# A drain between two tiny operations removed, and the start of the kernel reordered, in an attention and feed-forward layer

## The chip, the cores and the metric

The kernel runs on all 8 cores of one Trainium2 chip. Each core takes half the query tiles of one of the four batch entries (every other tile of 128 rows) and reads all keys of that entry that it needs; the cores exchange nothing. The metric is the device time in microseconds of the slowest core. The time before is 1715.69 us, the median of 3 runs (1714.91 to 1715.86).

## The reference, cut to what matters

```python
x = layernorm(x + attn(x, Wq, Wk, Wv, Wo))          # x: (4, 8192, 1024), float32
x = layernorm(x + ffn(x, U1, V1, b1, U2, V2, b2))

attn:  q, k, v = x@Wq, x@Wk, x@Wv;  scores = q @ k^T, causal mask
       softmax(scores / 32) @ v @ Wo
ffn:   gelu(x @ U1 @ V1 + b1) @ U2 @ V2 + b2        # rank 256, hidden width 4096
layernorm: (x - mean) / sqrt(var + 1e-5)
```

## The kernel before

Two products of weights are formed once on each core: M (`m_sb`) from Wq and Wk, and W (`wvo`) from Wv and Wo. With them the scores of a block of 512 queries are z = M x, then z x^T, and the attention's output is (P x) W. Both products are 1024 by 1024 and are computed in two column halves, h = 0 and h = 1, of 8 tiles (e = 0 to 7, 128 rows by 512 columns, 8 matmuls each).

**The start.** SP loads f32 pieces of 512 KB: 16 pieces of Wq and Wk (the list `QK`), 8 of x (own x and the other half of the first block), 16 of Wv and Wo (the list `VO`). ScalarE takes every other piece and casts it to bf16 (`cast`, L759), VectorE takes the rest (L838); their orders are `BY_ACT` and `BY_DVE`. A piece of `VO` from the ninth on reuses the staging place of the piece eight before it, so SP waits for that cast (L430). TensorE forms the first half of M row by row of the weights as they land (`product_by_rows`, L509), the second half tile by tile (`product_by_tiles`, L521), turns 8 tiles of x by transposes for each of the two key chunks (L605, copied out by ScalarE L774 and VectorE L908), then computes z of block 0 (8 tiles, L531), its scores (L547), and the first half of W (L521 again).

**The loop** runs over g = 0 to 7 blocks of 512 queries. Block g meets 2g + 2 key chunks of 512, in the order 2g, 2g + 1, 0, 1, ... (`score_chunks`). In one turn TensorE computes the scores that are left (L547), transposes the probabilities (L563), multiplies with the values (L579) and with W (L652), computes z of the next block (tiles 0 to 5, L531), transposes the first LayerNorm's output (L669), z tile 6, the FFN's first product (L681), z tile 7, the hidden layer (L692, L700), the scores of the next block against its first chunk, and the last product (L722).

**LayerNorm.** VectorE adds the residual to each W tile out of PSUM (L955), takes the statistics of each 128 rows (`statistics`: drain L874, `bn_stats` L876, drain L877, `bn_aggr` L878), and GpSimd computes 1/sqrt(var + eps) from the variance: an add of eps (L362), a drain (L364), a power of -0.5 (L365), each on 128x1 elements. VectorE then waits for it and normalizes (L881). `ln1_out(g, j - 1)` stands in VectorE's program between the residual adds of rows j and j + 1, so that VectorE empties no more W tiles while it waits for GpSimd. TensorE uses 6 PSUM banks as a ring: a new tile has to wait until the tile six before it has been copied out. For the second LayerNorm the statistics and norms are spread over the row maxima of the next block (`ln2_piece`).

**The queues.** Key chunks c >= 2 and all values are f32 in HBM and are cast to bf16 copies in HBM (`xtb`, `xnb`) by DMAs that GpSimd issues (`cast_xt` L329, 1 MB written each; `cast_xn` L332, 2 MB written each). Between L337 and L358 GpSimd first waits for the last casts of `BY_ACT` and `BY_DVE`, then issues, in this order: key chunk 2, the FFN's weights (u1, v1, u2, v2, b1, b2, all counted on one semaphore `d_wf`), key chunk 3, the values of blocks 0 and 1. After the first LayerNorm of block g it issues key chunks 2g + 4 and 2g + 5 and the values of block g + 2 (L371 to L374). SP loads bf16 chunks and values into a ring of five slots of SBUF (`load_scores` L399, `load_values` L405), in order: for block 1 these are chunks 2, 3, 0, 1 and then the values, and each load waits for the cast of what it reads (L398, L449, L450).

The text gives times of core 6, the slowest of the profiled execution.

Of the kernel before, what the change touches and what calls it, by code (L numbers as in the profile page):

```python
# [41 lines left out]
def psum_numbers():  # L42
# [22 lines left out]
    product("m", 0, RB)  # L65
    product("m", 1, 8)
    for c in range(2):
# [3 lines left out]
    for f in range(8):  # L71
        z(0, f)
# [79 lines left out]
def pair_pieces(a, b):  # L152
    out = []
    for i in range(4):
        out += [(a, 2 * i, None), (b, 2 * i, 0), (a, 2 * i + 1, None)]
    return out + [(b, 2 * i, 1) for i in range(4)]


QK = pair_pieces("q", "k")
VO = pair_pieces("v", "o")  # L160
# [6 lines left out]
def build_program():  # L167
# [25 lines left out]
    with ctx:  # L193
# [26 lines left out]
        eps_s = E(nc.sbuf_tensor("eps_s", [128, 1], F32))  # L220
# [29 lines left out]
        d_wf, d_const = S("d_wf"), S("d_const")  # L250
# [73 lines left out]
        def _(g):  # L324
            g.memset(eps_s[:, :], EPS)
# [14 lines left out]
            for k in range(8):  # L340
                g.dma_start(out=u1_sb[:, k * 256:(k + 1) * 256],
                            in_=u1_d.ap()[k * 128:(k + 1) * 128, :]).then_inc(d_wf, 16)
            for rc in range(2):
                g.dma_start(out=v1_sb[:, rc * 4096:(rc + 1) * 4096],
                            in_=v1_d.ap()[rc * 128:(rc + 1) * 128, :]).then_inc(d_wf, 16)
            for fq in range(4):
                g.dma_start(out=u2_sb[:, fq * 2048:(fq + 1) * 2048].rearrange("p (f r) -> p f r", f=8),
                            in_=u2_d.ap()[fq * 1024:(fq + 1) * 1024, :].rearrange(
                                "(f p) r -> p f r", p=128)).then_inc(d_wf, 16)
            for rc in range(2):  # L350
                g.dma_start(out=v2_sb[:, rc * 1024:(rc + 1) * 1024],
                            in_=v2_d.ap()[rc * 128:(rc + 1) * 128, :]).then_inc(d_wf, 16)
            g.dma_start(out=b1_sb[:, :], in_=b1_d.ap()[:, :]).then_inc(d_wf, 16)
            g.dma_start(out=b2_sb[:, :], in_=b2_d.ap()[:, :]).then_inc(d_wf, 16)
# [114 lines left out]
        def _(t):  # L469
# [32 lines left out]
            def product_by_rows(name, lhs, rhs, arrived):  # L502

                banks = [claim((name, 0, e)) for e in range(8)]
                for k in range(8):
                    for p in arrived(k):
                        cast_done(t, p)
                    for e in range(8):
                        mm = t.matmul(ps[banks[e]][:, :],  # L509
                                      lhs[:, k * 1024 + e * 128:k * 1024 + (e + 1) * 128],  # L510
                                      rhs[:, k * 1024:k * 1024 + 512],
                                      start=(k == 0), stop=(k == 7))
                        if k == 7:
                            mm.then_inc(s_full if e < RB else s_acc, 1)

            def product_by_tiles(name, lhs, rhs, h):

                for e in range(8):
# [6 lines left out]
                    mm.then_inc(s_full, 1)  # L525
# [61 lines left out]
            def first_half(a, b):  # L587
                return lambda k: [(a, k, None)] + ([(b, k, 0)] if k % 2 == 0 else [])

            def second_half(b):  # L590
                for i in range(4):
                    cast_done(t, (b, 2 * i, 1))

            product_by_rows("m", wqt, wkt, first_half("q", "k"))
            second_half("k")
            product_by_tiles("m", wqt, wkt, 1)
            t.wait_ge(d_const, 32)
            for c in range(2):
# [22 lines left out]
            for g in range(NG):  # L621
# [19 lines left out]
                if g == 0:  # L641
                    second_half("o")
# [31 lines left out]
                if g == 0:  # L674
                    t.wait_ge(d_wf, 16 * 18)
# [8 lines left out]
                if more:  # L684
                    z_tile(g + 1, 7)

# [21 lines left out]
                for fc in range(32):  # L708
                    hidden(fc)
                    if fc >= 3:  # L710
# [334 lines left out]
```

## Time and profile before

| | |
|---|---|
| time, median of 3 runs | 1715.69 us |
| the profiled execution's own time | 1717.22 us |
| its span on the slowest core (core 6) | 1715.7 us |
| spans of the 8 cores | 1708.8 to 1715.7 us |
| TensorE busy in matmuls | 1573.1 us (92%) |
| VectorE, ScalarE, GpSimd busy | 656.8, 615.3, 112.2 us |
| granted TensorE clock, core 6 | 0.975 of full speed |

Times in the profile count from the start of the core's span. An engine's row gives start, length, engine, line, operation and how many are merged; in brackets stands how long the engine had been idle and which instruction released it. POOL is GpSimd, DVE VectorE, ACT ScalarE, PE TensorE, SPq and POOLq the sequencers of SP and GpSimd. The DMA queue q0 holds what GpSimd issues, q1 what SP issues.

### The profile page before, as it was taken

Reading aid. Unit: us, or ns where it says so; the run is one execution under the profiler, and the core shown is the slowest. Engines: PE = TensorE matmul, PEld = TensorE weight load, DVE = VectorE, ACT = ScalarE, POOL = GpSimd, SP = SyncE. Lnnn points to the kernel's source line nnn. Section 1 sums busy time; section 2 is a strip of 40 time slices with the busy share of each in tenths; the row PEclk is TensorE's granted clock in tenths of the full one; section 3 lists DMA queues with packets and bytes.
Section 4 is the critical chain, followed back from the end, with each engine's and each line's share of the span. In section 5 each row is a group of like instructions: output and inputs, shape, how many; then the busy total and the mean of one; then the engine's idle time right before and its main releaser. Section 6 shows DMA issues by size and latency. Waiting matters only on the chain.

```text
span 1715.7 us, 26161 instructions; the slowest of 8 cores (1708.8 to 1715.7 us)
## 1 busy us (share of the span) xinstructions
PE 1573.1 (92%) x8608; PEld 774.1 (45%) x8608; DVE 656.8 (38%) x1318; ACT 615.3 (36%) x1242; POOL 112.2 (7%) x204
## 2 busy tenths in 40 slices
PE   6991499999999999999999999999999999999985
PEld 2540144444444544445444454444454444455432
DVE  2430325545416432652416440544540515461053
ACT  3510163354074306441074420354420264441023
POOL 0020101110101000100101000100000001000000
PEclk9996699999999999999999999999999999999998
DMA  9999755834665357524575335636335305434301
GB/s 296 306 141 133 131 87 192 164 86 155 202 87 195 106 192 99 167 92 136 200 95 188 132 110 210 110 87 203 129 118 203 134 26 197 148 109 147 137 1 49
DMA packets 72141, 244.55 MB, mean 143 GB/s; under 512 B 4992, under 2 KB 10256, under 8 KB 61328
## 3 DMA queue, kind: packets, MB, share of 16 engines
q1 hardware_dynamic: 60320, 190.86, 32.7%
q0 software_dynamic: 11696, 52.02, 19.6%
q8 instruction: 79, 1.29, 0.3%
q14 instruction: 46, 0.38, 0.1%
HBM read 258.69 MB, written 52.43 MB: 181 GB/s over the span
## 4 chain that ended last, share of the span: by engine, by line
PE 86%; issue 6%; DVE 3%; ACT 2%; DVEq 1%; SPq 1%; DMA 1%; POOLq 0%; POOL 0%; ACTq 0%
PE ps L579 27%; PE ps L547 26%; PE ps L700 7%; PE ps L692 6%; PE ps L531 6%; PE ps L652 5%; PE ps L563 3%; PE ps L521 3%; PE ps L681 2%; PE ps L722 2%; ACT p_sb L808 1%; SPq L423 1%; DMA x_ring<-wkt 1%; DVE p_sb L857 1%; PE ps L669 1%
## 5 line engine op out<-in xcount | busy, mean ns | idle before, releaser
L579 PE MATMUL ps<-p_sb,x_ring 128*128 128x512 bf16 (+2 forms) x2304 | 468.2, 361 | 8.9 <-DVE p_sb L864 5.7
L547 PE MATMUL ps<-x_ring,zt 128*128 128x512 bf16 (+3 forms) x2304 | 465.1, 361 | 0.8 <-ACT zt L732 0.8
L547 PEld LDWEIGHTS ps<-x_ring,zt 128*128 128x128 bf16 x2304 | 220.2, 98 | 235.4 <-issue 1.3
L579 PEld LDWEIGHTS ps<-p_sb,x_ring 128*128 128x128 bf16 x2304 | 216.9, 98 | 235.0 <-issue 11.6
L742 ACT ACTIVATE p_sb<-ps,nm 128x512 bf16<-128x512 f32 (+3 forms) x288 | 187.3, 651 | 264.6 <-DVE nm L846 264.5
L846 DVE TENSOR_REDUCE nm<-ps 128x1 f32<-128x512 f32 (+3 forms) x288 | 184.5, 643 | 202.4 <-PE ps L547 202.4
L823 ACT ACTIVATE p_sb<-ps,b_sb 128x512 bf16<-128x512 f32 x256 | 171.4, 688 | 37.6 <-PE ps L692 35.7
L531 PE MATMUL ps<-x_ring,p_sb 128*128 128x512 bf16 x512 | 116.1, 383 | 60.2 <-DVE x L955 58.7
L700 PE MATMUL ps<-p_sb,wf 128*128 128x512 bf16 x512 | 148.4, 379 | 9.5 <-ACT p_sb L823 9.5
L945 DVE CAST ot<-ps 128x512 bf16<-128x512 f32 x32 | 22.1, 692 | 342.0 <-PE ps L579 342.0
L692 PE MATMUL ps<-p_sb,wf 128*128 128x512 bf16 x512 | 148.5, 379 | 0.6 <-ACT p_sb L732 0.6
L732 ACT ACTIVATE zt<-ps 128x512 bf16<-128x512 f32 x64 | 38.8, 607 | 261.4 <-PE ps L531 261.4
L732 ACT ACTIVATE ot<-ps 128x512 bf16<-128x512 f32 x32 | 19.1, 597 | 287.9 <-PE ps L579 287.9
L970 DVE CAST q_sb<-ps 128x512 bf16<-128x512 f32 x16 | 10.3, 686 | 281.1 <-PE ps L700 281.1
L362 POOL TENSOR_TENSOR vpe<-mv,eps_s 128x1 f32<-128x1 f32 x64 | 22.1, 346 | 1422.6 <-DVE mv L878 1422.6
L793 ACT ACTIVATE p_sb<-ps 128x512 bf16<-128x512 bf16 (+1 forms) x144 | 77.1, 571 | 100.1 <-PE ps L563 100.0
L652 PE MATMUL ps<-wvo,ot 128*128 128x512 bf16 x512 | 111.8, 379 | 1.2 <-DVE wvo L834 1.2
L531 PEld LDWEIGHTS ps<-x_ring,p_sb 128*128 128x128 bf16 x512 | 49.9, 99 | 121.5 <-issue 64.3
L563 PE MATMUL ps<-idb,p_sb 128*128 128x128 bf16 x1056 | 72.5, 219 | 16.7 <-DVE p_sb L857 16.2
L876 DVE BATCH_NORM_STATS2 bst<-x 128x6 f32<-128x512 f32 x128 | 82.3, 685 | 5.8
L857 DVE TENSOR_SCALAR p_sb<-p_sb,fac 128x512 bf16<-128x512 bf16 (+3 forms) x288 | 82.8, 337 | 0.0
L700 PEld LDWEIGHTS ps<-p_sb,wf 128*128 128x128 bf16 x512 | 50.0, 98 | 72.2 <-issue 14.7
(66 smaller groups left out, 955.6 us busy)
## 6 DMA issues: line engine op xcount, KB each, us to landing
x_ring<-xtb SPq DMA_DIRECT2D x70, 1024.0 KB, 6.5
x_ring<-xnb SPq DMA_DIRECT2D x48, 1024.0 KB, 5.4
x<-xo SPq DMA_DIRECT2D x32, 512.0 KB, 8.5
xnb<-xn POOLq DMA_DIRECT2D x8, 2048.0 KB, 35.1
xtb<-xt POOLq DMA_DIRECT2D x14, 1024.0 KB, 18.5
out<-x POOLq DMA_DIRECT2D x28, 512.0 KB, 8.2
x_ring<-xnb SPq DMA_DIRECT2D x16, 768.0 KB, 5.0
x_ring<-xnb SPq DMA_DIRECT2D x16, 512.0 KB, 4.3
```

Source lines behind the costliest of these rows:

```text
L531: mm = t.matmul(ps[b][:, :], m_sb[:, ec * 1024 + f * 128:ec * 1024 + (f + 1) * 128], ring[:, off + ec * 512:off + (ec + 1) * 512], start=( ...
L547: mm = t.matmul(ps[b][:, 0:w], zt[:, ec * 512 + j * 128:ec * 512 + (j + 1) * 128], ring[:, off + ec * 512:off + ec * 512 + w], start=(ec = ...
L563: mm = t.transpose(psb[b][:, k * 128:(k + 1) * 128], P[:, p0:p0 + 128], idb[:, :])
L579: mm = t.matmul(ps[b][:, q0:512], ring[:, off + k * step:off + k * step + 128], P[:, p0 + q0:p0 + 512], start=(c == 0 and k == 0), stop=(c ...
L652: mm = t.matmul(ps[b][:, :], ot[:, e * 512 + j * 128:e * 512 + (j + 1) * 128], wvo[:, e * 1024 + h * 512:e * 1024 + (h + 1) * 512], start= ...
L692: mm = t.matmul(ps[b][:, :], v1_sb[:, rc * 4096 + fc * 128:rc * 4096 + (fc + 1) * 128], p1_sb[:, rc * 512:(rc + 1) * 512], start=(rc == 0) ...
L700: mm = t.matmul(ps[b][:, :], u2_sb[:, fc * 256 + rc * 128:fc * 256 + (rc + 1) * 128], h_sb[:, (fc % 8) * 512:(fc % 8 + 1) * 512], start=(f ...
L742: sc.activation(blocks(c, j, w // 128), b[:, 0:w].rearrange("p (n k) -> p n k", k=128), AF.Exp, bias=nm[:, k:k + 1], scale=1.0, accum_out= ...
L823: sc.activation(h_sb[:, (fc % 8) * 512:(fc % 8 + 1) * 512], b[:, :], AF.Gelu_apprx_tanh, bias=b1_sb[:, fc:fc + 1]).then_inc(out_of["gelu"], 1)
L846: v.tensor_reduce(nm[:, k:k + 1], src[:, 0:width(g, c, j)], AX.X, ALU.max, negate=True).then_inc(s_nm, 1)
L857: v.tensor_scalar(pv, pv, fac[:, j * 16 + ti:j * 16 + ti + 1], None, ALU.mult).then_inc(s_scaled, 1)
L876: v.bn_stats(bst[:, j * 12 + h * 6:j * 12 + (h + 1) * 6], half(j, h))
```

## The change

1. In `rstd_of` GpSimd's add and drain are removed; VectorE adds eps itself (a drain and a 128x1 `tensor_scalar` behind `bn_aggr`, in `statistics`). GpSimd keeps the power alone.
2. M is formed in four quarters. All pieces of Wq and Wk are now halves of two rows' columns, in the order in which the quarters need them; quarters 1 to 3 are formed by rows as pieces land, quarter 4 by tiles. M's tiles are copied out between the casts. Two of M's last tiles go to the other two PSUM banks.
3. Own x (chunk 0) is turned first, then 6 tiles of z are computed, then chunk 1 is turned, then z tiles 6 and 7.
4. The casts of Wv and Wo pieces move: several now stand between the exponentials (ScalarE) and the row maxima (VectorE) of block 0's scores.
5. ScalarE does a tiny activation before its first cast.
6. The FFN's weights have semaphores of their own (`d_u1`, `d_v1` with b1, `d_u2`, `d_v2` with b2), b1 is loaded ahead of v1, and each use in block 0 waits for its own.

```diff
             def rstd_of(col, s_mv, s_rs, n):
                 g.wait_ge(s_mv, n)
-                g.tensor_tensor(vpe[:, col:col + 1], mv[:, 2 * col + 1:2 * col + 2],
-                                eps_s[:, :], ALU.add)
-                g.drain()
                 g.tensor_tensor(rstd[:, col:col + 1], vpe[:, col:col + 1],
                                 mhalf[:, :], ALU.pow).then_inc(s_rs, 1)
...
-                v.bn_aggr(mv[:, 2 * col:2 * col + 2], bst[:, j * 12:j * 12 + 12]).then_inc(s_mv, 1)
+                v.bn_aggr(mv[:, 2 * col:2 * col + 2], bst[:, j * 12:j * 12 + 12])
+                v.drain()
+                v.tensor_scalar(vpe[:, col:col + 1], mv[:, 2 * col + 1:2 * col + 2], EPS, None,
+                                ALU.add).then_inc(s_mv, 1)
...
-QK = pair_pieces("q", "k")
-VO = pair_pieces("v", "o")
+QK = [(a, 2 * i, 0) for i in range(4) for a in "qk"]
+QK += [("q", 2 * i, 1) for i in range(4)] + [("k", 2 * i, 1) for i in range(4)]
...
+            product_by_rows("m", wqt, wkt, 0, range(4), ("q", 0, "k", 0))
+            product_by_rows("m", wqt, wkt, 0, range(4, 8), ("q", 1))
+            product_by_rows("m", wqt, wkt, 1, range(4), ("k", 1))
+            product_by_tiles("m", wqt, wkt, 1, range(4, 8))
+            t.wait_ge(d_const, 32)
+            turned_x(0)
             for f in range(8):
...
+                if f == 6:
+                    turned_x(1)
                 z_tile(0, f)
...
+            sc.activation(recip[:, 0:1], nc.const_aps.tensor(0.0, (128, 1)), AF.Copy)
+            for i, p in enumerate(BY_ACT[0:8]):
+                cast(p)
+                if i == 4:
+                    product_out("m", m_sb, SCALE, 0, (0, 2))
+                if i == 6:
+                    product_out("m", m_sb, SCALE, 0, (4, 6))
+            product_out("m", m_sb, SCALE, 1, (0, 2, 4))
+            cast(BY_ACT[8])
+            product_out("m", m_sb, SCALE, 1, (6,))
+            cast(BY_ACT[9])
+            turned_x(0)
+            for f in range(6):
                 z_out(0, f)
-                if f < 6:
-                    cast(BY_ACT[12 + f])
+                if f in (1, 3):
+                    cast(BY_ACT[10 + f // 2])
+            turned_x(1)
+            cast(BY_ACT[12])
+            z_out(0, 6)
+            cast(BY_ACT[13])
+            z_out(0, 7)
             for ti in range(2):
-                exps(0, ti)
+                for jj in range(2):
+                    exps(0, ti, (2 * jj, 2 * jj + 1))
+                    cast(BY_ACT[14 + 2 * ti + jj])
...
-            for p in BY_DVE[12:18]:
+            turned_x(0)
+            for p in BY_DVE[10:12]:
+                cast(p)
+            turned_x(1)
+            for p in BY_DVE[12:15]:
                 cast(p)
             for ti in range(2):
                 for j in range(4):
                     row_max(0, ti, j)
+                    if j % 2 == 1 and (ti, j) != (1, 3):
+                        cast(BY_DVE[15 + 2 * ti + j // 2])
             for p in BY_DVE[18:]:
                 cast(p)
...
                 if g == 0:
-                    t.wait_ge(d_wf, 16 * 18)
+                    t.wait_ge(d_u1, 16 * 8)
```

## Rows read from the trace of the kernel before

**Rows 1.** The waits of 120 to 200 us: total, times, longest.

```profile
DVE p_sb L881 <- POOL rstd L365: 64.9, 1, 64.9
PE ps L531 <- DVE x L955: 58.7, 1, 58.7
```

**Rows 2.** GpSimd's drain, min, median and longest in ns.

```profile
L364 POOLq DRAIN  x64: 266/607/67495, 125.8 to 1708.0; - x64
```

**Rows 3.** Timeline of GpSimd (start, length, operation), 82 to 194 us.

```profile
82.87 0.63 POOL L329 DMA_DIRECT2D xtb<-xt  x1 [79.74 <-DVE p_sb L840]
...
94.99 1.19 POOL L332 DMA_DIRECT2D xnb<-xn  x2
...
125.85 0.19 POOL L362 TENSOR_TENSOR vpe<-mv,eps_s 128x1 f32<-128x1 f32 x1 [29.67 <-DVE mv L878]
193.40 0.56 POOL L365 TENSOR_TENSOR rstd<-vpe,mhalf 128x1 f32<-128x1 f32 x1 [67.37 <-issue]
```

**Rows 4.** SP's waits of 96 to 200 us: total, times, longest.

```profile
SPq L449 <- DMA xnb<-xn: 18.6, 1, 18.6
SPq L450 <- DMA xnb<-xn: 18.5, 1, 18.5
```

**Rows 5.** SP's three loads of chunks 3, 0, 1, issued 153.8 to 154.8 us.

```profile
DMA to landing us min/median/max: 38.7/40.6/42.5
```

**Rows 6.** The two DMA queues, 158 to 182 us: packets, MB, share of 16 engines.

```profile
q0 software_dynamic: 85, 2.26, 83.1%
q1 hardware_dynamic: 80, 0.66, 10.8%
```

**Rows 7.** DMA issues, with us to landing: values 2 (204.73 us), b2 (93.97 us).

```profile
xnb<-xn POOLq DMA_DIRECT2D x1, 2048.0 KB, 34.8
...
b_sb<-b2b POOLq DMA_DIRECT2D x1, 512.0 KB, 50.5
```

**Rows 8.** Timeline of TensorE's matmuls, the start.

```profile
33.32 16.85 PE L521 MATMUL ps<-p_sb 128*128 128x512 bf16 x64 [5.00 <-ACT p_sb L732]
50.01 3.79 PE L605 MATMUL ps<-idb,x_ring 128*128 128x128 bf16 x64
54.50 13.97 PE L531 MATMUL ps<-x_ring,p_sb 128*128 128x512 bf16 x64 [0.70 <-DVE x_ring L908]
69.83 0.41 PE L547 MATMUL ps<-x_ring,zt 128*128 128x128 bf16 x2 [0.27 <-ACT zt L732]
...
78.60 13.98 PE L521 MATMUL ps<-p_sb 128*128 128x512 bf16 x64
```

**Rows 9.** The stretch 195 to 198 us: engines busy, PEclk, DMA share, GB/s.

```profile
195.00:198.00 3.00, 2.31 (x6) 0.87 (x7) 2.84 (x6) 0.00 (x0) 0.29 (x1) 0.50 0.26 100
```

**Rows 10.** Timelines of ScalarE and VectorE, the start.

```profile
31.63 1.06 ACT L761 ACTIVATE p_sb<-x_ring 128x1024 bf16<-128x1024 f32 x1 [2.20 <-DMA x_ring<-wkt]
...
80.34 0.28 ACT L748 ACTIVATE fac<-nm,nmf 128x2 f32<-128x2 f32 x1
...
79.83 2.50 DVE L840 CAST p_sb<-wf 128x1024 bf16<-128x1024 f32 x4
```

**Rows 11.** Timeline of TensorE's matmuls, blocks 0 and 1.

```profile
119.56 13.97 PE L652 MATMUL ps<-wvo,ot 128*128 128x512 bf16 x64 [1.16 <-DVE wvo L834]
...
204.51 2.37 PE L669 MATMUL ps<-idb,p_sb 128*128 128x128 bf16 x32
...
252.14 0.22 PE L547 MATMUL ps<-x_ring,zt 128*128 128x128 bf16 x1
...
255.20 15.49 PE L547 MATMUL ps<-x_ring,zt 128*128 128x512 bf16 x71
...
300.20 13.98 PE L652 MATMUL ps<-wvo,ot 128*128 128x512 bf16 x64
...
324.37 2.36 PE L669 MATMUL ps<-idb,p_sb 128*128 128x128 bf16 x32
```

**Rows 12.** VectorE, a small operation: busy us, mean ns, idle before.

```profile
L850 DVE TENSOR_REDUCE nmf<-nm 128x1 f32<-128x2 f32 (+7 forms) x32 | 5.2, 163 | 3.5 <-issue 0.5
```

More of the change, by code:

```diff
@@ L63, in scores, with turned_x @@
                 put(ring, ring_out, ("s", g, t, j), "exp")
-    product("m", 0, RB)
-    product("m", 1, 8)
-    for c in range(2):
+    def turned_x(c):
         for j in range(4):
@@ L70, in psum_numbers @@
                 put(ring, ring_out, ("x0", c, j, h), "x0_act" if h == 0 else "x0_dve")
-    for f in range(8):
+    product("m", 0, RB)
+    product("m", 1, RB)
+    turned_x(0)
+    for f in range(6):
+        z(0, f)
+    turned_x(1)
+    for f in range(6, 8):
         z(0, f)
@@ L147, in load_count @@
     return n // SLOTS + (1 if n % SLOTS >= MADE else 0)
[L152 to L156, printed above, removed]
-QK = pair_pieces("q", "k")
-VO = pair_pieces("v", "o")
+QK = [(a, 2 * i, 0) for i in range(4) for a in "qk"]
+QK += [("q", 2 * i, 1) for i in range(4)] + [("k", 2 * i, 1) for i in range(4)]
+VO = []
+for _i in range(4):
+    VO += [("v", 2 * _i, None), ("o", 2 * _i, 0), ("v", 2 * _i + 1, None)]
+VO += [("o", 2 * _i, 1) for _i in range(4)]
 BY_ACT = QK[1::2] + [("x", b, None) for b in (1, 3, 5, 7)] + VO[1:12:2]
@@ L585, in values_chunk, with turned_x @@
                     mm.then_inc(s_unit, 1)
[L587 to L598, printed above, removed]
+            def turned_x(c):
                 for j in range(4):
@@ L641, in _ @@
                 if g == 0:
-                    second_half("o")
+                    for i in range(4):
+                        cast_done(t, ("o", 2 * i, 1))
                     product_by_tiles("w", wvt, wo_sb, 1)
@@ L709, in _ @@
                     hidden(fc)
+                    if g == 0 and fc == 3:
+                        t.wait_ge(d_u2, 16 * 4)
                     if fc >= 3:
@@ L732, in copy_out, with exps @@
                 sc.activation(dst, src[:, :], AF.Copy, scale=scale).then_inc(out_of[by], 1)
-            def exps(g, ti):
+            def exps(g, ti, js=range(4)):
                 c = score_chunks(g)[ti]
-                for j in range(4):
+                for j in js:
                     w = width(g, c, j)
@@ L895, in ln2_piece, with turned_x @@
                     norm(row(j), j, 4 + j).then_inc(s_ln2, 1)
[L897 to L904 removed]
+            def turned_x(c):
                 for j in range(4):
@@ L910, in _ @@
                                   ).then_inc(out_of["x0_dve"], 1)
-            for p in BY_DVE[12:18]:
+            for i, p in enumerate(BY_DVE[0:8]):
+                cast(p)
+                if i == 4:
+                    product_out("m", m_sb, SCALE, 0, (1, 3))
+                if i == 6:
+                    product_out("m", m_sb, SCALE, 0, (5, 7))
+            product_out("m", m_sb, SCALE, 1, (1, 3))
+            cast(BY_DVE[8])
+            product_out("m", m_sb, SCALE, 1, (5,))
+            cast(BY_DVE[9])
+            product_out("m", m_sb, SCALE, 1, (7,))
+            turned_x(0)
+            for p in BY_DVE[10:12]:
+                cast(p)
+            turned_x(1)
+            for p in BY_DVE[12:15]:
                 cast(p)
```

70 lines of the change are left out of this document (30 added, 40 removed).

## The prediction

> **What bounds the kernel now.** The page comes first: TensorE is busy in 92% of the span and the chain that ended last runs through its matmuls, so whatever opens or closes a gap in TensorE's row moves the end. I therefore looked for the gaps. The list of waits has one that is larger than all the others together: 58.7 us in which TensorE's z matmuls of block 1 waited for VectorE's residual add [rows 1]. Followed back, VectorE waited 64.9 us for GpSimd's power [rows 1], and the power itself sat 67.4 us with "issue" as its reason [rows 3]: it waited for nothing but the instruction ahead of it. That instruction is the drain: its median is 0.6 us, its longest 67.5 us [rows 2]. GpSimd's timeline shows the setting: from 82.87 to 96.2 us it issues its DMAs, the add at 125.85 us takes 0.19 us, the power comes at 193.40 us [rows 3]. SP saw the last of these DMAs, the values of block 1, land at 192.3 us (its waits L449 and L450 follow each other, 18.6 and 18.5 us, after the load at 154.8 us: 154.8 + 0.4 (its issue) + 18.6 + 18.5 [rows 4, 5]). So the drain waits until all that GpSimd has queued has landed. In the other seven blocks nothing is in flight when LayerNorm comes, and the drain costs under a microsecond.
>
> **The second resource in that stretch is the DMA queue.** From 158 to 182 us q0 (GpSimd's casts) moves 2.26 MB in 85 packets and q1 (SP's loads) 0.66 MB in 80 packets [rows 6]. The two take turns packet by packet, but a packet of q0 has 27 KB and one of q1 8 KB, so q1 gets 0.66/24 = 27 GB/s while q0 has work. The three loads of 1 MB each that SP issued at 153.8 to 154.8 us take 38.7 to 42.5 us, that is until q0 runs dry [rows 5]. Before, this cost nothing: TensorE needs chunk 3 at 252.14 us only [rows 11]. What the drain's wait held up was also GpSimd's next three casts (chunks 4 and 5, values of block 2), which took up to 34.8 us to land, alone on the engines [rows 7].
>
> **Part 1, the start.** The last piece of Wk is cast at 31.63 + 1.06 = 32.7 us [rows 10] and loads are what paces this, so that stays. Before, half of M (64 matmuls) is left then and ends at 33.32 + 16.85 = 50.2 us; the same 64 take 13.98 us later [rows 8], so 2.9 us of it are a clock that had fallen while TensorE waited, and the new order has no such wait. After, 8 matmuls of quarter 3 and 32 of quarter 4 are left: 40 x 0.218 us (13.98/64) = 8.7, end 41.4 us. Turning one chunk costs half of the 54.50 - 50.17 us plus the last copies, some 2.7 us: z starts at 44.1 us. Eight z tiles (13.97 us) and the second turn (1.9 us, half of L605) end at 60.0 us; the scores then wait for the copy of z tile 7 behind two casts on ScalarE, to 60.7 us, against 69.83 us: 9.1 us gained. Here the change adds a wait. W needs all casts of its first half of pieces; the last one now stands on ScalarE behind the last exponential. Before, ScalarE is through with these at 80.34 + 0.28 = 80.6 us [rows 10]; 9.1 earlier is 71.5, the cast takes 1.06, and the casts ahead of it in the same loop delay it by about 1 more: 73.6 us, against 78.6 us for W's first matmul [rows 8]. Of the 9.1 us, 5.0 are left on TensorE. Bounds: 9 if the casts are hidden, 2 if the late pieces of Wv and Wo land later, since SP's loads now wait for casts that are later in both engines' programs. I take 5, from the order above. GpSimd's queue opens when VectorE has cast the last piece, 79.83 + 2.50 = 82.3 us before; after, about 75 to 77 us, and it then shares the engines with SP's stores, so I count 6 us for the whole of q0 (bounds 3 and 9).
>
> **Part 2, the drain.** Without it the power runs as the add did, 0.2 to 0.6 us, with DMAs in flight. The stretch from W's product (119.56, less 5) to the transposes of LayerNorm's output takes in block 0 what it takes in block 1, 324.37 - 300.20 = 24.2 us [rows 11], so the transposes come at 138.7 instead of 204.5 us. From there to the scores against chunk 3 is 252.14 - 204.51 = 47.6 us: TensorE asks for chunk 3 at 186.4 us, 65.8 us earlier than before. The last of the FFN's weights, b2, lands at 93.97 + 50.5 = 144.5 us [rows 7], less 6, and is first asked for at about 141 us; so edit 6 is free, covered by the z tiles and LayerNorm; it would cost up to 3 us if q0 ran 15 us later.
>
> **Part 3, what is late next.** Chunk 3's cast landed at 153.7 us; 6 earlier it is 147.7, and 1.05 MB at 27 GB/s is 39 us: chunk 3 is there at about 187 to 188 us, TensorE loses 1 to 2 us and is through with it at 193 (4.8 us of matmuls). Now it needs chunk 0. But GpSimd, no longer held, issues its three casts at about 133 us, behind the rest of q0 and without a gap. q0 would have ended at 192.3 - 6; to that come 4.2 MB. Values 0 and 1, 2.1 MB each, took 18.6 us each beside q1 [rows 4], so 4.2 MB take 37 to 38 us: q0 ends at about 224 us. By then q1 has moved 27 GB/s x 72 us = 1.9 MB of the 2.1 MB that chunks 3 and 0 need, and chunk 0 lands a microsecond or two behind q0's end, at 225.5 us; chunk 1 follows at q1's full rate, in time. TensorE stands still from 193 to 225.5 us and starts again at half clock, as it did at 195 us (0.50 [rows 9]), which costs 1.9 us over four tiles (8.8 for 6.9). Two chunks of four 512-wide tiles are 13.8 us: the scores of block 1 end at 241.2 us instead of 255.20 + 15.49 = 270.7 us [rows 11]. **Gain 29.5 us.** The values of block 1 are cast before that and load in time. Note that part 1's gain on TensorE drops out of this sum; only the earlier opening of q0 counts.
>
> The Trainium skill (DMA: Bandwidth & Descriptors, Anatomy of one DMA) gives a DMA from GpSimd as 2.0 us plus bytes over 436 GB/s; by that the three casts would take some 16 us, q0 would end near 202 us and the time would be near 1665 us. The row of this case, 34.8 us for them alone [rows 7], speaks against it.
>
> **Part 4, VectorE.** Each of 64 statistics gets a drain and a small operation, 0.16 us by its like [rows 12] plus about 0.1 for the drain. In blocks 0 to 6 z's tiles cover it (5 us of slack between the last norm and the transposes in block 1). In block 7 no z follows, and the last LayerNorm ends the kernel: twice (4 x 0.26 - 0.8) = +0.5 us, where 0.8 is GpSimd's add (0.19 [rows 3]) and its median drain (0.61 [rows 2]). If VectorE's extra work were on the path in every block it would be up to 17 us (64 x 0.26), if all is hidden the removed 0.8 is a small gain.
>
> **The sum.** 1717.2 (profiled execution) - 29.5 + 0.5 = 1688.2 us. The median of the runs is 1.5 us under the profiled execution, so 1687 us. Its own bounds: q0 opening 3 to 9 us earlier, casts of 35 to 45 us: 1677 to 1699.
>
> **Rivals.**
> (B) The queue doesn't starve SP: chunks 3, 0, 1 come in time. Then the whole stall goes: 58.7 + 1.9 (clock) + 5.0 - 0.5, and 1 less for VectorE's longer work in block 1: 1717.2 - 64 - 1.5 = 1652 us. It needs q1 at 50 GB/s or more, twice what the row shows. The Trainium skill (same page, Queues, rings and completion order) has each engine change rows at packet borders, and its section SWDGE vs HWDGE vs iDMA has packets of at most 4096 B preferably; equal packets would halve the rate between the queues and bring this case about. The trace differs: 27 KB against 8 KB [rows 6]. Chance 0.12, and 0.10 for something between B and the forecast.
> (C) The change doesn't do what it says: the power itself, or its semaphore, waits for what is queued, as the drain did. For it: the add, which ran at 125.85 us, carries no semaphore. Against it: it is the same kind of instruction on the same engine, and it ran. The stall would end with q0, 6 us earlier: 1717.2 - 6 + 0.5 - 1.5 = 1710 us. Chance 0.09.
> (D) Slower: as C, but GpSimd's queue opens later than before. Its opening waits for the last casts, which the change moves behind row maxima and exponentials, and SP's loads of the last eight pieces wait for earlier casts in turn. From then on everything up to 193 us moves one for one with that opening. It decides if the last cast ends after 83 us; at 86 us the time is 1717.2 + 3.7 + 0.5 - 1.5 = 1720 us. My order gives 76 us. Chance 0.03.
>
> **How the numbers follow.** Forecast 0.66 at 1687 us. The range takes the forecast's bounds, the cases between and B: 1652 to 1699 us. It leaves out C and D and the edges. A measurement of this kernel tells 0.2% (3.4 us) from no change. Faster: 0.66 + 0.22 + half of C; same: the rest of C; slower: D. That is 0.93, 0.04 and 0.03.
>
> **What would show it.** In the trace of the changed kernel: no drain on GpSimd and a power of about 0.55 us near 121 us; GpSimd's casts of chunks 4 and 5 near 133 us; the first half of M's copies between casts, z from 44 us, W's first product at 73.6 us with a wait for a cast on ScalarE; TensorE's longest wait in the scores of block 1, for the load of chunk 0, 25 to 35 us long, with q1 near 27 GB/s until then. I am wrong in part 3 if TensorE runs through from 186 us; in part 2 if the power starts near 187 us; in part 1 if W's product starts before 70 or after 77 us.

## The result, and the profile after

The changed kernel is faster: the ratio to the kernel before is 0.9907, 95% interval 0.9888 to 0.9927, that is about 1699.4 us against 1715.3 us (with a fourth run the median of the kernel before is 1715.3 us, not 1715.69). (The median of its four executions, 1723.78 us, contains two in which the cores of one die ran at a lower clock; the other two took 1699.22 and 1700.61 us, and all that follows compares undisturbed runs.) The gain is 16 us. Forecast were 28 us, with 1687 us as the time and 1699 us as the upper end of the range: the direction and the chain of waits came out. The term for the reordered start did not: it was counted as a gain and is a loss. The time lies just above the range.

The profiled execution took 1699.22 us; its slowest core is now core 2, with 1697.7 us. Its waits from 0 to 330 us (who waited for whom, total, times, longest):

```profile
POOL rstd L363 <- DVE vpe L899: 163.0, 12, 66.2
...
PE ps L547 <- DMA x_ring<-xtb: 39.9, 2, 27.8
...
PE ps L521 <- ACT p_sb L767: 3.5, 1, 3.5
```

The 58.7 us for VectorE's residual add [rows 1] are gone. In their place stands one line of TensorE that did not exist before: 39.9 us in two waits for the loads of key chunks. GpSimd's timeline answers [rows 3]:

```profile
77.68 0.54 POOL L330 DMA_DIRECT2D xtb<-xt  x1 [74.62 <-DVE p_sb L859]
...
89.80 1.18 POOL L333 DMA_DIRECT2D xnb<-xn  x2
124.38 0.56 POOL L363 TENSOR_TENSOR rstd<-vpe,mhalf 128x1 f32<-128x1 f32 x1 [33.40 <-DVE vpe L899]
...
136.77 1.78 POOL L330 DMA_DIRECT2D xtb<-xt  x2
138.54 0.74 POOL L333 DMA_DIRECT2D xnb<-xn  x1
```

The power runs at 124.38 us in 0.56 us, with all of the queue still in flight, and the next three casts go out at 136.8 to 139.3 us instead of 203 us. SP's side (waits of 60 to 330 us, and the three loads of chunks 3, 0, 1, issued 159.2 to 160.4 us, from issue to landing) answers [rows 4, 5]:

```profile
SPq L448 <- DMA xnb<-xn: 21.5, 1, 21.5
SPq L447 <- DMA xnb<-xn: 18.4, 1, 18.4
```

```profile
DMA to landing us min/median/max: 42.5/75.9/80.5
```

Chunk 3 takes 42.5 us, but chunk 0 now 75.9 and chunk 1 80.5 us, where before all three were there within 42.5. Chunk 3's cast itself has landed only when SP issues the first of these loads, at 159.2 us; on core 6 before that was 153.8 us, and 147.7 was forecast. And the reason is in the queues' shares, here from 160 to 180 us (packets, MB, share), to be read beside [rows 6]:

```profile
q0 software_dynamic: 77, 2.00, 87.2%
q1 hardware_dynamic: 55, 0.45, 10.2%
```

q1 has 22 GB/s while q0 has casts (22 to 32 GB/s on the eight cores). TensorE's timeline of blocks 0 and 1, the counterpart of [rows 11]:

```profile
117.86 13.97 PE L651 MATMUL ps<-wvo,ot 128*128 128x512 bf16 x64 [1.16 <-DVE wvo L853]
131.67 10.52 PE L531 MATMUL ps<-x_ring,p_sb 128*128 128x512 bf16 x48
142.03 2.36 PE L668 MATMUL ps<-idb,p_sb 128*128 128x128 bf16 x32
...
201.88 0.27 PE L547 MATMUL ps<-x_ring,zt 128*128 128x128 bf16 x1 [12.13 <-DMA x_ring<-xtb]
...
235.79 15.54 PE L547 MATMUL ps<-x_ring,zt 128*128 128x512 bf16 x64 [27.75 <-DMA x_ring<-xtb]
```

It waits 12.1 us for chunk 3 and 27.8 us for chunk 0. The scores of block 1 end at 251.3 us. Behind that nothing has moved up to the last block: block 1's transposes to block 7's W product take 1364.7 us (252.84 to 1617.58), on core 6 before 1364.8 (272.23 to 1637.05).

### The profile page after: what moved, and what is told of

Same layout as the page of the kernel before. It is cut to its first block, busy times and chain, and to the rows that moved or that the text cites. A ratio compares the mean times of both kernels' runs of the same rounds, so it can differ in the third digit from the quotient of the medians.

```text
span 1697.7 us, 26164 instructions; the slowest of 8 cores (1686.8 to 1697.7 us)
## 1 busy us (share of the span) xinstructions
PE 1575.0 (93%) x8608; PEld 775.1 (46%) x8608; DVE 669.5 (39%) x1382; ACT 614.8 (36%) x1243; POOL 98.6 (6%) x139
## 4 chain that ended last, share of the span: by engine, by line
PE 83%; another core or an unknown queue 5%; DMA 5%; ACT 2%; DVE 2%; issue 2%; DVEq 0%; SPq 0%; ACTq 0%; POOLq 0%
PE ps L547 27%; PE ps L579 26%; PE ps L702 6%; PE ps L694 6%; PE ps L651 6%; PE ps L531 5%; PE ps L563 3%; DMA x_ring<-xtb 3%; PE ps L680 2%; PE ps L728 1%; DMA xtb<-xt 1%; ACT p_sb L827 1%; PE ps L509 1%; DMA wf<-wkt 1%
## 5 line engine op out<-in xcount | busy, mean ns | idle before, releaser
L547 PE MATMUL ps<-x_ring,zt 128*128 128x512 bf16 (+3 forms) x2304 | 468.0, 363 | 40.3 <-DMA x_ring<-xtb 39.9
L579 PEld LDWEIGHTS ps<-p_sb,x_ring 128*128 128x128 bf16 x2304 | 217.0, 98 | 234.9 <-issue 11.5
L748 ACT ACTIVATE p_sb<-ps,nm 128x512 bf16<-128x512 f32 (+3 forms) x288 | 187.1, 651 | 305.6 <-DVE nm L865 305.5
L363 POOL TENSOR_TENSOR rstd<-vpe,mhalf 128x1 f32<-128x1 f32 x64 | 47.5, 743 | 1469.9 <-DVE vpe L899 1469.9
L702 PEld LDWEIGHTS ps<-p_sb,wf 128*128 128x128 bf16 x512 | 50.0, 98 | 72.2 <-issue 14.7
L563 PEld LDWEIGHTS ps<-idb,p_sb 128*128 128x128 bf16 x1056 | 64.6, 97 | 35.7 <-issue 21.1
```

What stands on the lines that cost most here:

```text
L547: mm = t.matmul(ps[b][:, 0:w], zt[:, ec * 512 + j * 128:ec * 512 + (j + 1) * 128], ring[:, off + ec * 512:off + ec * 512 + w], start=(ec = ...
L563: mm = t.transpose(psb[b][:, k * 128:(k + 1) * 128], P[:, p0:p0 + 128], idb[:, :])
L579: mm = t.matmul(ps[b][:, q0:512], ring[:, off + k * step:off + k * step + 128], P[:, p0 + q0:p0 + 512], start=(c == 0 and k == 0), stop=(c ...
L702: mm = t.matmul(ps[b][:, :], u2_sb[:, fc * 256 + rc * 128:fc * 256 + (rc + 1) * 128], h_sb[:, (fc % 8) * 512:(fc % 8 + 1) * 512], start=(f ...
L748: sc.activation(blocks(c, j, w // 128), b[:, 0:w].rearrange("p (n k) -> p n k", k=128), AF.Exp, bias=nm[:, k:k + 1], scale=1.0, accum_out= ...
```

## The experiments

Two questions were open. Why is the gain 12 us smaller than forecast? The candidates were the start (theory Q: its reordering makes the cast queue q0 late; rival S: it gives its 5 us and the loss is elsewhere). And is it packet turns that starve SP's loads, or is the memory as a whole the limit? Twelve kernels were run, each against the kernel before; the ratio stands with its 95% interval. The kernel before was run again beside each group, and its median is not the same in all: 1715.3 us beside the change, 1716.9 beside e1 to e4, 1719.3 beside e6 to e9, 1716.1 beside e10 to e13. Where kernels of two groups are compared, the difference is therefore given as a range, from the times themselves and from the ratios times 1715.3 us. "Values 1" is the time at which the cast of block 1's values has landed, the lowest and highest of the eight cores; it is when SP issues the first load of values. Before: 185.4 to 192.4 us; in the changed kernel 188.5 to 201.0 us.

| kernel | ratio to before | slowest core's span, us | values 1, us |
|---|---|---|---|
| the change | 0.9907 (0.9888 to 0.9927) | 1697.7 | 188.5 to 201.0 |
| e1 drain only | 0.9880 (0.9863 to 0.9897) | 1693.8 | 185.6 to 195.7 |
| e2 start only | 1.0033 (1.0019 to 1.0047) | 1719.9 | 190.2 to 195.7 |
| e3 casts held | 0.9845 (0.9828 to 0.9862) | 1688.2 | 189.8 to 196.9 |
| e4 chunk 3 first | 0.9878 (0.9854 to 0.9902) | 1694.8 | 196.5 to 207.5 |
| e6 store of M late | 0.9844 (0.9824 to 0.9863) | 1690.6 | 182.7 to 190.6 |
| e7 small rows | 0.9797 (0.9775 to 0.9819) | 1682.8 | 198.8 to 212.3 |
| e8 held and split | 0.9798 (0.9779 to 0.9818) | 1685.1 | 188.6 to 198.7 |
| e9 e8 and store late | 0.9994 (0.9955 to 1.0032) | 1712.2 | 181.9 to 188.4 |
| e10 e7 and store late | 0.9809 (0.9792 to 0.9826) | 1682.8 | 190.8 to 207.1 |
| e11 e10 on the old start | 0.9810 (0.9790 to 0.9829) | 1679.5 | 190.8 to 212.0 |
| e12 casts before the scores | 0.9865 (0.9846 to 0.9885) | 1690.2 | 184.9 to 187.6 |
| e13 e10 and e12 | 0.9780 (0.9748 to 0.9812) | 1676.1 | 187.1 to 203.1 |

### The parts of the change, one at a time

**e1, the kernel before with the drain removed.**

```diff
-                g.tensor_tensor(vpe[...], mv[...], eps_s[:, :], ALU.add)
-                g.drain()
                 g.tensor_tensor(rstd[...], vpe[...], mhalf[:, :], ALU.pow).then_inc(s_rs, 1)
...
-                v.bn_aggr(mv[...], bst[...]).then_inc(s_mv, 1)
+                v.bn_aggr(mv[...], bst[...])
+                v.drain()
+                v.tensor_scalar(vpe[...], mv[...], EPS, None, ALU.add).then_inc(s_mv, 1)
```

> The kernel before with edit 1 alone (drain and add off GpSimd, eps added by VectorE). Theory Q (the cast queue q0 is what block 1 waits for, and the reordered start makes q0 later although it opens earlier): values 1 land where they did before, 185 to 192 us, block 1's first transposes come 55 us behind that as in the changed kernel (240 to 247 us, 25 us earlier than before), and the time is 1688 to 1694 us, less than the 1699 us of the full change. Rival S (the start brings the 5 us that the forecast gave it, and the shortfall lies in the drain's part): this kernel is 5 us or more slower than the full change, 1704 us or more.

Measured: 0.988, 1695.5 us in the median, against 1699.4 us for the full change. One edit of six gives at least as much as all six; that it gives more is likely and not certain, since the intervals (0.9863 to 0.9897, 0.9888 to 0.9927) overlap a little. The time is 1.5 us above what theory Q said and 8.5 us below what rival S needs. Values 1 and the transposes came later than theory Q said on some cores: 185.6 to 195.7 us and 241.4 to 249.9 us.

**e2, the change with the add and the drain back on GpSimd.**

```diff
                 g.wait_ge(s_mv, n)
+                g.tensor_tensor(vpe[...], mv[...], eps_s[:, :], ALU.add)
+                g.drain()
                 g.tensor_tensor(rstd[...], vpe[...], mhalf[:, :], ALU.pow).then_inc(s_rs, 1)
...
-                v.drain()
-                v.tensor_scalar(vpe[...], mv[...], EPS, None, ALU.add).then_inc(s_mv, 1)
```

> The changed kernel with GpSimd's add and drain back as before: the start and the weights' semaphores alone. Theory Q: the power waits again for the end of q0, which now comes at 188 to 201 us instead of 185 to 192 us, so the kernel is slower than before, 1718 to 1726 us. Rival S: q0 ends 6 us earlier, 1710 us.

Measured: 1.0033, 1721.7 us, slower than the kernel before by 5 to 6 us, as theory Q said. GpSimd's timeline (its slowest core, 5):

```profile
81.77 0.54 POOL L332 DMA_DIRECT2D xtb<-xt  x1 [78.63 <-DVE p_sb L864]
...
123.88 0.18 POOL L365 TENSOR_TENSOR vpe<-mv,eps_s 128x1 f32<-128x1 f32 x1 [28.81 <-DVE mv L902]
196.71 0.56 POOL L368 TENSOR_TENSOR rstd<-vpe,mhalf 128x1 f32<-128x1 f32 x1 [72.64 <-issue]
```

The drain holds the power until 196.7 us, 3.3 us later than on the slowest core before, although LayerNorm comes 2 us earlier. On all 16 cores of this kernel and of the kernel before, the power starts 1.0 us behind the landing of values 1, the last thing that GpSimd has queued; that is what shows for what the drain waits. So the reordered start is worth about -4 to -6 us by itself, where the forecast had +5 (TensorE) and +6 (queue). What it gives TensorE, a W product at 75 instead of 78 us, nobody can use.

### Why the queue that opens earlier ends later

The bytes of the two queues from 77 to 110 us, on core 2 before and in the changed kernel:

```profile
q0 software_dynamic: 1398, 3.06, 72.0%
q1 hardware_dynamic: 249, 2.61, 24.1%
```

```profile
q0 software_dynamic: 1331, 2.47, 54.7%
q1 hardware_dynamic: 382, 3.78, 49.6%
```

q0 opens at 77.7 instead of 81.8 us, but SP's last weight loads and its stores of x and M now go out at 62 to 72.5 us instead of up to 66, and 1.2 MB more of q1 fall into the stretch. The engines are full in both kernels; q0 has moved 0.6 MB less. The other cores agree: q0 moves 2.66 to 3.42 MB there before and 2.24 to 2.69 MB in the changed kernel.

Why SP is later is seen ahead of the opening. q1's row from 40 to 62 us, on core 2 before, on core 2 in the changed kernel, and on core 5 in e12 (described below):

```profile
q1 hardware_dynamic: 2337, 6.64, 92.4%
```

```profile
q1 hardware_dynamic: 2011, 5.90, 79.9%
```

```profile
q1 hardware_dynamic: 2514, 7.33, 99.1%
```

In the changed kernel a fifth of the engines' time passes unused there (8% before), since SP waits for a cast that frees a staging place (one wait of 16.3 us for VectorE, 15.7 to 16.4 us on the other cores; 12.5 us on core 2 before, and 4.6 us at the longest on core 5 in e12). So the loads and stores that the engines could have done then are done beside q0 instead. Two experiments take load off this stretch in two ways.

**e6, the store of M moved** from ahead of SP's loop over the blocks to behind block 1's loads of values and x.

```diff
-            s.dma_start(out=mscr.ap()[:, :], in_=m_sb).then_inc(d_ms, 16)
             for g in range(1, NG):
...
+                if g == 1:
+                    s.dma_start(out=mscr.ap()[:, :], in_=m_sb).then_inc(d_ms, 16)
```

> The changed kernel with SP's store of M (2 MB, issued at 71 us, first read in block 7) moved behind block 1's loads. Theory O: the cast queue q0 is late in the changed kernel because it opens at 77 us into SP's loads and stores (issued 62 to 73 us, 6 us later than before), which share the engines with it until about 100 us. Without this store values 1 land 5 to 8 us earlier (median of the cores 192 to about 186 us) and the time is 1691 to 1694 us. Rival: the lateness has another source (the neighbour core's traffic, the order of the weights); values 1 move by under 2 us and the time stays at 1698 to 1700 us.

Measured: values 1 at 182.7 to 190.6 us, the time 1692.9 us, ratio 0.9844, as theory O said, though values 1 come 4.5 us earlier in the median of the cores where 5 to 8 were expected. The gain over the change is 6.5 us by the times and 11 us by the ratios; the intervals lie apart.

**e12, edit 4 undone.** The store of M stays; the casts of Wv and Wo stand ahead of the exponentials and row maxima again.

```diff
             for f in range(6):
                 z_out(0, f)
-                if f in (1, 3):
-                    cast(BY_ACT[10 + f // 2])
+                if f < 5:
+                    cast(BY_ACT[10 + f])
...
+            for p in BY_ACT[15:18]:
+                cast(p)
             for ti in range(2):
-                for jj in range(2):
-                    exps(0, ti, (2 * jj, 2 * jj + 1))
-                    cast(BY_ACT[14 + 2 * ti + jj])
+                exps(0, ti)
...
```

VectorE's casts move likewise, from between its row maxima to ahead of them.

> The changed kernel with edit 4 undone: the casts of Wv and Wo stand ahead of block 0's exponentials and row maxima again. Theory O: SP's last loads and its stores then go out near 62 us instead of 70 to 72 us and are through before GpSimd's queue opens (near 75 us); values 1 land 5 to 8 us earlier than in the changed kernel (median 192.3 us to 184 to 188 us), the 3.5 us wait ahead of W's product is gone, and the time is 1691 to 1694 us. Rival: where the casts stand makes no difference to the queue, since the same bytes are moved by then: values 1 within 2 us of 192 us, 1698 to 1700 us.

Measured: 0.9865, 1692.9 us, values 1 at 184.9 to 187.6 us on all cores. SP's timeline (core 5), and the same stretch 77 to 110 us:

```profile
64.88 1.10 SPq L433 DMA_DIRECT2D xtb<-x_ring  x2
66.14 0.65 SPq L436 DMA_DIRECT2D mscr<-p_sb  x1
94.23 52.82 SPq L397 DMA_DIRECT2D x_ring<-xtb  x4
186.57 10.16 SPq L403 DMA_DIRECT2D x_ring<-xnb  x3
```

```profile
q0 software_dynamic: 1437, 3.14, 69.4%
q1 hardware_dynamic: 240, 2.36, 32.9%
```

The stores go out 6 us earlier, q0 moves 0.67 MB more in the stretch (slowest core against slowest core), and block 1's first transposes come at 241.7 to 244.3 us; the forecast for them was 242.7 (its 241.2 us for the end of the scores, and 1.5 us between the two as on core 6 before). The place of these casts carries 6.5 to 7 of the missing 12 us. The head start is still not worth the 6 us written: against the kernel before, values 1 come 4.8 us earlier on the slowest core (187.6 against 192.4 us) and 1.3 us in the median of the cores.

### Why SP's loads starve beside the casts

**e3, the three casts behind block 0's second LayerNorm.**

```diff
-                if gi + 2 < NG:
-                    cast_xt(2 * gi + 4)
-                    cast_xt(2 * gi + 5)
-                    cast_xn(gi + 2)
+                def next_casts():
+                    if gi + 2 < NG:
+                        cast_xt(2 * gi + 4)
+                        cast_xt(2 * gi + 5)
+                        cast_xn(gi + 2)
+                if gi > 0:
+                    next_casts()
                 for j in range(4):
                     rstd_of(4 + j, s_mv2, s_rs2, 4 * gi + j + 1)
+                if gi == 0:
+                    next_casts()
```

> The changed kernel, with the three casts that GpSimd issues after block 0's first LayerNorm (chunks 4 and 5, values 2) issued behind its second one instead (near 200 us). Theory Q with packet turns (SP's loads crawl at 27 GB/s as long as casts are queued): q0 is empty at 188 to 201 us, chunk 3 lands then and chunks 0 and 1 within 5 us behind it; TensorE's wait for chunk 0 (28 us) falls under 3 us, the one for chunk 3 (0 to 12 us) stays; block 1's transposes come 25 to 30 us earlier, near 222 us on the slowest core, and the time is 1668 to 1674 us. Rival B (the memory as a whole is the limit and the order doesn't matter): the wait shrinks by under 10 us and the time stays at 1690 us or more.

Measured: 0.9845, 1690.1 us; a gain of 9 to 11 us over the change, not 27. The time is the rival's, though not its reason, since the wait for chunk 0 did go. The waits of its slowest core, 120 to 330 us:

```profile
PE ps L584 <- DMA x_ring<-xnb: 21.8, 1, 21.8
...
PE ps L552 <- DMA x_ring<-xtb: 6.9, 1, 6.9
```

The part on chunk 0 came out: its 27.8 us are gone, and TensorE runs from chunk 3 through chunks 0 and 1 without a break. But the casts, now issued at 208 to 211 us, meet the loads of block 1's values, which SP issues from 197 to 234 us on that core, most of them behind the casts, and TensorE waits 15 to 25 us there (all cores). I had counted the wait that I took away and not the next user of the same queue.

**e4, chunk 3 cast ahead of the FFN's weights.**

```diff
             cast_xt(2)
+            cast_xt(3)
             for k in range(8):
                 g.dma_start(out=u1_sb[...], ...)
...
-            cast_xt(3)
             cast_xn(0)
```

> The changed kernel with key chunk 3 cast ahead of the FFN's weights. Theory Q: chunk 3's cast lands near 115 us, its load and that of chunk 0 go beside the weights' small packets and are done by 150 us, chunk 1 by 190 us, so the waits for key chunks (33 to 40 us on TensorE) fall under 8 us; but values 1 still land at 190 to 200 us and their loads then crawl beside the new casts, 19 us for each half MB, so a new wait of 15 to 30 us opens at block 1's values: 1680 to 1692 us. VectorE waits about 20 us for b2, hidden. Rival B: the wait only moves, 1697 us or more.

Measured: 0.9878, 1695.7 us, between what theory Q (up to 1692) and the rival (1697 or more) said; that the wait only moves was the rival's word. No wait for key chunks is left; TensorE waits 26 to 31 us for values instead, and up to 8.7 us for u2.

**e7, the same casts in shorter rows.**

```diff
+                if c in (3, 4, 5):
+                    for i in range(4):
+                        g.dma_start(out=xtb.ap()[c][:, i * 1024:(i + 1) * 1024],
+                                    in_=xt_d.ap()[c][:, i * 1024:(i + 1) * 1024]).then_inc(d_ct[c], 16)
+                    return
                 g.dma_start(out=xtb.ap()[c], in_=xt_d.ap()[c]).then_inc(d_ct[c], 16)
```

The casts of values 0, 1 and 2 are cut likewise, into two halves of their rows.

> The changed kernel with the casts of chunks 3, 4, 5 in four column parts and of values 0, 1, 2 in two, the same bytes in shorter rows (4 KB and 2 KB of f32 instead of whole contiguous stretches). Theory P (the engines change queues packet by packet, so SP's rate beside casts is set by the size of q0's packets, 27 to 33 KB against 8 KB): q0's packets shrink, SP's loads run at 50 GB/s or more beside them, TensorE's wait for chunk 0 (28 us) falls under 12 us, 1675 to 1688 us. Rival (q1's rate is what the memory leaves, whatever the packets): 27 GB/s and the waits as before, 1697 us or more.

Measured: 0.9797, 1684.4 us, within what theory P said. The queues from 160 to 180 us (core 2), to be held against 77 and 55 packets in the changed kernel:

```profile
q0 software_dynamic: 1089, 1.09, 51.0%
q1 hardware_dynamic: 410, 2.97, 47.2%
```

q0's packets are 1 KB now instead of 26 KB, and q1's share of the engines' time goes from 10 to 47%, its rate from 22 to 149 GB/s. (On cores 1, 5 and 7 it is 46 to 49%; on the other four SP's loads were issued 4 to 8 us earlier and q1 has 98 to 114 GB/s over this stretch.) The bytes and their order are the same; the number of DMAs is larger, four or two for each cast instead of one, and no run separates that from the shorter rows. All three key chunks are there in time: on core 2 their loads take 13.8 to 21.2 us instead of 42.5 to 80.5. The price: q0 moved 1.09 instead of 2.00 MB, values 1 come at 199 to 212 us, and the values' loads cost TensorE 13 to 22 us. What is left, a gain of 15 to 19 us over the change, is what serving both queues at once is worth; the bytes stay.

**e8, e3's idea with more care**: chunk 4 behind the second LayerNorm, chunk 5 and values 2 behind the landing of block 1's last value load.

```diff
-                if gi + 2 < NG:
+                if 0 < gi < NG - 2:
...
+                if gi == 0:
+                    cast_xt(4)
...
+                if gi == 0:
+                    n = STREAM[("v", 1, 7, 0)]
+                    g.wait_ge(d_slot[n % SLOTS], 16 * load_count(n))
+                    cast_xt(5)
+                    cast_xn(2)
```

> The changed kernel with chunk 4's cast behind block 0's second LayerNorm and those of chunk 5 and values 2 behind the landing of block 1's last value load. Holding all three only until the second LayerNorm removed the wait for chunk 0 (28 us) but opened one of 15 to 24 us at block 1's values, whose loads then met the casts. Theory Q: here the values' loads meet 1 MB of casts only; the wait at the values falls to 0 to 10 us, chunk 3's (0 to 7 us) stays, 1672 to 1680 us, if chunk 4, 5 and values 2 still come in time for block 2. Rival: the bytes are merely too many for this stretch, and a new wait of 10 us or more opens in block 2 or at block 1's LayerNorm (x is loaded behind the values): 1685 us or more.

Measured: 0.9798, 1685.4 us: the rival's number. The waits of the slowest core, 120 to 420 us:

```profile
PE ps L554 <- DMA x_ring<-xtb: 8.9, 1, 8.9
PE ps L538 <- DMA x_ring<-xtb: 8.8, 1, 8.8
PE ps L658 <- DVE x L995: 8.3, 1, 8.3
```

The wait at the values is gone; the first row is the wait for chunk 3, which stays as expected. In place of the other TensorE waits for chunk 4 at z of block 2 (L538, up to 22.4 us on another core) and for VectorE, which waits for x at block 1's LayerNorm (L658).

**e9, e8 with the store of M late**, the diffs of e8 and e6 together.

> e8_hold_split and e6_m_store_late together. If both theories hold the 5 to 8 us of the earlier q0 end the wait for chunk 3 and let the values start earlier: 1667 to 1675 us, 4 us or more under e8. If TensorE no longer waits for q0 in e8, it is as fast as e8.

Measured: 0.9994, 1718.6 us where 1667 to 1675 were expected: all the gain lost. On the slowest core (1), its wait of 120 to 420 us, and of its DMA issues of 225 to 245 us the store and the load of chunk 4 (KB each, us to landing):

```profile
PE ps L538 <- DMA x_ring<-xtb: 55.9, 1, 55.9
```

```profile
mscr<-p_sb SPq DMA_DIRECT2D x1, 2048.0 KB, 54.7
x_ring<-xtb SPq DMA_DIRECT2D x1, 1024.0 KB, 79.6
```

The same store that helped in e6 is issued here among the held casts, just ahead of chunk 4's load on SP's queue: its 2 MB take 54.7 us and the load behind it 79.6. Core 2 waits 36.0 us in the same place; the other six wait at most 13.1 us there and have spans of 1683 to 1685 us. The store alone does not make this difference, for it takes 45 to 47 us on those cores too, and chunk 4's load 49 to 50 us (35 to 47 us in e8). What differs is when GpSimd issues the casts for block 3: at 262.1 us on core 1 and 270.3 us on core 2, where the load lands at 307.7 and 296.2 us, but at 275 to 289 us on the six, where it lands at 278 to 282 us. On these two cores the late load meets the next casts and crawls once more. The expectation missed this entirely.

**e10, e7 with the store of M late**, the diffs of e7 and e6 together.

> e7_small_rows and e6_m_store_late together. In e7 TensorE waits 13 to 22 us for block 1's values, whose casts land at 199 to 212 us; the store of M out of the way brought them 5 us forward. Theory: values 1 land 5 us earlier, the wait falls by as much, 1677 to 1681 us. Rival: the store only takes the same time from block 1's loads later (it goes behind them, ahead of block 2's): no gain, 1684 to 1687 us.

Measured: 0.9809, 1684.1 us, the same as e7 within the intervals. The waits for values fell to 5 to 11 us, but on most cores 2 to 6 us for chunk 4 and up to 3 at LayerNorm came instead: the rival.

**e11, e10 on the start of the kernel before**, the diffs of e1, e6 and e7 together on that kernel.

> As e10, but on the start of the kernel before (edits 2 to 6 of the change left out). If the reordered start is worth the 2 to 3 us by which W's first product begins earlier, now that the queue holds TensorE less, this is 2 to 5 us slower than e10. If its earlier opening of the queue is worth nothing, since the engines are full from the first load on and only the bytes count, the two are within 2 us.

Measured: 0.981, 1684.8 us, e10's ratio. So beside e10's two changes the reordered start is worth nothing that these runs can tell.

**e13, the diffs of e7, e6 and e12 together.**

> e10_small_rows_store_late with e12's order of the casts: the three edits that helped, together. If what each gives the cast queue adds up (q1 has less to move beside it after 77 us, TensorE starts W 3 us earlier), TensorE's remaining waits in blocks 1 and 2 (10 to 20 us in e10) shrink by 3 to 5 us: 1677 to 1681 us. If the engines are simply full until about 250 us, it is within 2 us of e10's 1684 us.

Measured: 0.978 (0.9748 to 0.9812), the lowest ratio of all, 1677.7 us and as expected, with 12.4 us of waiting for values left on its slowest core. It beats the change clearly (0.9907); that it beats e7, e8, e10 or e11 is not shown, since the intervals overlap.

## Why the prediction was right or wrong, point by point

**The drain** [rows 2, 3]: right. It waits until all that GpSimd has issued has landed (e2); the power with its semaphore does not. Rivals C and D are out: 0.56 us at 124.38 us. **That the stall turns into a wait for chunk 0**: right, 27.8 us where 32 were written. **q1's rate**: 27 GB/s written, 22 measured. **The casts' issue** near 133 us: 136.8. Rival B is out as the kernel stands; e7 shows that the size of q0's packets was the right condition to name. The Trainium skill (DMA: Bandwidth & Descriptors, Queues, rings and completion order) has each engine change rows at packet borders. The traces agree in direction: q1 has 10% of the time beside q0's packets of 26 KB and 47% beside packets of 1 KB. But the prediction's "packet by packet" is not shown as a strict turn: 77 to 55 packets in the changed kernel, 1089 to 410 in e7. The Trainium skill (DMA: Bandwidth & Descriptors, SWDGE vs HWDGE vs iDMA) has packets of at most 4096 B preferably; the contiguous casts of this trace, at 26 KB a packet, do not keep to that.

**The step that failed** is the term "I count 6 us for the whole of q0 (bounds 3 and 9)" of part 1. The queue did open 3.3 to 6.7 us earlier, as forecast. But the end of its first load, the landing of values 1, was to come at 186.3 us on the slowest core and came at 201.0; the forecast took the head start as if the engines had been idle before the opening. They were not idle at the opening, but still busy with q1; and edit 4, part of the same reordering, had left them a fifth unused from 40 to 62 us and pushed SP's stores later, by 6 us, into q0's time: 1.2 MB more of q1 from 77 to 110 us. Of the 14.7 us, 11.5 are there already when chunk 3's cast lands, at 159.2 us where 147.7 was forecast; the casts that the drain no longer holds stand behind it in the queue. I wrote "it then shares the engines with SP's stores" and gave it no price. e6 and e12 give it: 6.5 us of the time each by the times (1692.9 against 1699.4), 11 and 7 us by the ratios; their intervals end below that of the change. e12, which has the head start and not the late stores, has its transposes within 1.6 us of the forecast. Its time is still 6 us above the forecast of 1687: 3.5 us in the profiled execution (1691.7 against 1688.2), of which 1.5 come before the transposes and 2 behind them, and the rest because the median of its runs lies 1.2 us above its profiled execution and not 1.5 us below.

The remainder of the sum, on the slowest core: the scores of block 1 end at 251.3 instead of 241.2 us (10.1 us). That consists of the 14.7 us by which values 1 are late, less 4.4 us by which the three new casts, and with them chunk 0, followed more quickly (34.8 us from values 1 to chunk 0, where 39.2 were written); the matmuls behind chunk 0 make up the rest. The other 0.9 us of the 11.0 by which the span is above the forecast's come behind block 1's scores, VectorE's part below. TensorE's wait for chunk 3, 12.1 us where 1 to 2 were written, and its asking for it at 189.8 instead of 186.4 us cost nothing by themselves, for chunk 0 ends the wait in either case. The last core of one kernel is not that of the other; on core 6 alone the change brought 26 us, on core 2 11 us, and the slowest decides.

**VectorE's extra work**: right in kind, small in size. The four statistics at the end stand 0.23 us further apart each (1687.57 to 1688.10 from `bn_aggr` to the next statistics, before 1702.72 to 1703.02). From block 7's W product to the end it is 80.1 us instead of 78.7: 1.5 us, where 0.5 was written. Twice four times 0.23 us are 1.8 us, so by this estimate the forecast's 0.8 us for GpSimd's removed work, counted twice, came back only in small part; no run separates it.

```profile
1687.57 0.21 DVE L897 BATCH_NORM_AGGREGATE mv<-bst 128x2 f32<-128x12 f32 x1
1687.85 0.15 DVE L899 TENSOR_SCALAR vpe<-mv 128x1 f32<-128x1 f32 x1
1688.10 1.29 DVE L895 BATCH_NORM_STATS2 bst<-x 128x6 f32<-128x512 f32 x2
```

**The start on TensorE**: M ended at 42.8 us (41.4 written), z began at 45.5 (44.1), W's product at 75.3 (73.6) with 3.5 us of waiting for a cast on ScalarE, as named. Of the 5.0 us that were to be left on TensorE, 1.7 reached the second W product of block 0 (117.86 against 119.56 us), for the first took 15.6 us behind that wait (granted clock 0.76 from 72 to 78 us) and not 14.0. **The weights' own semaphores**: b2 made VectorE wait 9.0 us, hidden. That the start's gain on TensorE drops out of the sum was right, and is why nothing of it shows.

**The range** was too narrow upwards for the same reason: its upper end took a head start of 3 us as the worst case, and a loss was not among the bounds, though the prediction itself named the sharing with SP's stores.

What stays open: why e6, by the ratios, gives more than e12, and how much of the cores' spread in one kernel (12.5 us in the end of values 1) comes from the neighbour core; the profile shows one core's queues at a time and no run here separates it.

## What to carry to other kernels

When a stall is removed, ask which resource worked through it. Here the DMA engines were full during the whole 67 us, so the stall was their time as much as GpSimd's; what is late next is the same queue, and moving a transfer only changes who waits for it (chunk 0, values, chunk 4, in turn). And a queue that opens earlier ends earlier only as far as the engines have room for it: add up the bytes of all queues, and look for time that the engines lose ahead of the opening, not at the opening times.

## What the runs showed of the hardware

- GpSimd's drain waits for all DMAs that it has issued, 67.5 us at the longest; on 16 cores of two kernels the power behind it started 1.0 us after the last of them had landed. The power with a semaphore ran in 0.56 us beside the same DMAs.
- While casts of contiguous f32 data (26 to 27 KB a packet) were queued, SP's loads (8 KB a packet) got 22 to 32 GB/s in the changed kernel; with the casts cut to packets of 1 KB they got 149 GB/s on the slowest core, and the casts fell from 100 to 55 GB/s. The expectation was 50 GB/s or more.
- An edit that only moved casts on two engines (e12 against the change) brought forward the time at which block 1's values were cast: 188.5 to 201.0 us (lowest and highest core) became 184.9 to 187.6 us.
